# Sending the row of maxima to its place from ScalarE's queue

## The reference

```
h      = group_norm(x)                     # 32 groups of 6 channels, per sample
q,k,v  = h @ qkv_w + qkv_b                 # 12 heads x 16
attn   = (q * 16**-0.5) @ k.T + rel_h + rel_w   # rel_h, rel_w: q times a table, by row and by column
out    = softmax(attn) @ v
x      = x + out @ proj_w + proj_b
```

## Time and profile before

| | |
|---|---|
| median of three runs (lowest to highest) | 3290.96 us (3282.64 to 3295.18) |
| the profiled execution, its time and its span | 3282.28 us, 3280.5 us |
| instructions | 84768 |
| mean granted TensorE clock | 0.743 |
| transfers issued by SP for the row of maxima | 256, of 2.3 KB |

### The profile page before, as it was taken

The page is one execution under the profiler, slowest core; times in us unless marked ns, Lnnn a source line. Parts: engine busy times, 40 slices in busy tenths (PEclk is TensorE's granted clock), DMA queues, the critical chain, the costliest instruction groups (busy, mean ns, idle before and its releaser), DMA issues. The chain is left out here.

```text
span 3280.5 us, 84768 instructions
## 1 busy us (share of the span) xinstructions
PE 2706.0 (82%) x28288; PEld 1964.7 (60%) x28288; DVE 2205.2 (67%) x4041; ACT 2282.8 (70%) x4097; POOL 914.6 (28%) x2052
## 2 busy tenths in 40 slices
PE   2887988888888888878888888788888888888887
PEld 1565655566556656656666566566565655665665
DVE  4666766666666666666776666676667766666775
ACT  2677767767766677667777666777677777667775
POOL 1232222222222232223222222322322222223231
PEclk9877777767766786677677777777777776677787
DMA  2222222222222222222222222222222222222221
GB/s 54 61 76 63 67 70 69 62 65 74 68 62 62 66 76 64 62 66 75 65 75 69 62 67 68 71 61 68 72 65 62 72 71 62 63 67 75 62 76 40
DMA packets 170839, 217.61 MB, mean 66 GB/s; under 512 B 29935, under 2 KB 138220, under 8 KB 170446
## 3 DMA queue, kind: packets, MB, share of 16 engines
q1 hardware_dynamic: 170446, 211.93, 25.5%
HBM read 117.30 MB, written 57.80 MB: 53 GB/s over the span
## 5 line engine op out<-in xcount | busy, mean ns | idle before, releaser
L726 DVE TENSOR_REDUCE mx<-ps_max 98x2 f32<-98x392 f32 x1536 | 827.4, 558 | 515.7 <-PE ps_max L538 503.5
L780 DVE TENSOR_TENSOR rel_hl<-ps_m,rel_hi 64x504 f16<-64x504 f32 (+1 forms) x768 | 938.6, 1222 | 249.1 <-ACT rel_hi L666 232.3
L597 ACT ACTIVATE probs<-ps_sc 98x392 f32<-98x392 f32 x1536 | 739.3, 498 | 245.3 <-PE ps_sc L550 225.0
L569 PE MATMUL ps_o<-probs,v_st 98*32 98x196 f32 x6144 | 540.6, 434 | 268.6 <-ACT o_sb L590 246.2
L666 ACT ACTIVATE rel_hi<-ps_m,is_lo 64x504 f16<-64x504 f32 (+1 forms) x384 | 752.7, 1960 | 4.9
L538 PE MATMUL ps_max<-k_st,q_st 124*98 124x196 f16 x3072 | 660.4, 305 | 101.9 <-issue 91.3
L538 PEld LDWEIGHTS ps_max<-k_st,q_st 124*98 124x98 f16 x3072 | 333.0, 146 | 493.5 <-issue 401.1
L550 PE MATMUL ps_sc<-q_st,k_st 125*98 125x196 f16 x3072 | 626.2, 293 | 1.6 <-DMA q_st<-mrow 1.5
L550 PEld LDWEIGHTS ps_sc<-q_st,k_st 125*98 125x98 f16 x3072 | 411.7, 155 | 5.3 <-DMA q_st<-mrow 2.0
L822 POOL TENSOR_TENSOR xn_lo<-xn,xn_hi 96x392 f16<-96x392 f32 x128 | 118.8, 928 | 1005.3 <-ACT xn_hi L616 1005.3
L569 PEld LDWEIGHTS ps_o<-probs,v_st 98*32 98x32 f32 x6144 | 138.6, 123 | 428.8 <-issue 210.9
(11 more groups left out here) (71 smaller groups left out, 3957.9 us busy)
## 6 DMA issues: line engine op xcount, KB each, us to landing
q_st<-q_dram SPq DMA_DIRECT2D x128, 294.0 KB, 3.9
k_st<-k_dram SPq DMA_DIRECT2D x256, 147.0 KB, 3.0
q_dram<-qk_hl SPq DMA_DIRECT2D x128, 147.0 KB, 2.8
k_dram<-qk_hl SPq DMA_DIRECT2D x128, 147.0 KB, 2.8
q_st<-rel_hl SPq DMA_DIRECT2D x256, 73.5 KB
q_st<-rel_hl SPq DMA_DIRECT2D x256, 64.3 KB
xa<-in_x SPq DMA_DIRECT2D x64, 147.0 KB
xd<-in_x SPq DMA_DIRECT2D x64, 147.0 KB
```

The source lines that it names most:

```text
L569: last = nc.tensor.matmul(ps_o[32 * j:32 * j + 32, 0:TOK], v_st[u.r][:, kt, head_of(head), :], p[:, kt, :], start=kt == 0, stop=kt == 1)
L597: nc.scalar.activation(probs[head][:, :, :], ps_sc[head % 2][0:HT, 0:2 * TOK].rearrange("p (k t) -> p k t", k=2), ACT.Exp, scale=1.0 / (QS ...
L726: nc.vector.reduce_max(mx[u.r % 2][:, s, :], ps_max[s % 2][0:HT, 0:2 * TOK].rearrange("p (q k) -> p q k", q=2), axis=AX.X).then_inc(s_mx, 1)
L780: last = nc.vector.tensor_tensor(l, src, h, ALU.subtract)
```

## The change

The two transfers of `mrow` leave SP's queue. ScalarE issues them itself, right behind the instruction that writes `mrow`, after a wait for that instruction's own semaphore. Source, destination and the semaphores on which the landing is counted are the same. What follows on ScalarE's queue (`rel1` in slot 1, `xT` in slot 6) stands behind the transfer now, and SP no longer waits for `s_mrow`.

```diff
--- before (SP)
+++ after (SP)
-                def maxima(unit_, half):
-                    if active(unit_):
-                        wait(sp, s_mrow, unit_.n * 2 + half + 1)
-                        sp.dma_start(q_st[unit_.r][R_MAX:STACK, half * HH:half * HH + HH, :, :],
-                                     mrow[unit_.r % 2][:, half, :]).then_inc(s_m[half][unit_.r], 16)
...
-                maxima(c, 1)
                 if active(e):
                     wait(sp, s_rlo, e.n * 3 + 3)
...
                 if active(u):
                     wait(sp, s_qklo, u.n * NT + NT)
                     to_dram(u, q_dram, 0, s_qd)
-                maxima(m, 0)
                 if active(u):
                     to_dram(u, k_dram, HQ * HD, s_kd)
--- before (ScalarE)
+++ after (ScalarE)
                             nc.scalar.activation(mrow[u.r % 2][:, half, :], ps_m[BANK[name]][0:HEADS, 0:HT],
                                                  ACT.Copy, scale=-1.0 / KS).then_inc(s_mrow, 1)
+                            act.wait_ge(s_mrow, u.n * 2 + half + 1)
+                            act.dma_start(q_st[u.r][R_MAX:STACK, half * HH:half * HH + HH, :, :],
+                                          mrow[u.r % 2][:, half, :]).then_inc(s_m[half][u.r], 16)
```

## The result

The changed kernel takes 3391.03 us (median of 4 runs, 3381.86 to 3400.09) against 3288.66 us for the kernel before, run beside it: a ratio of 1.0306, 95% interval 1.0269 to 1.0344. The forecast was 3400 us and 1.033. The profiled execution took 3391.8 us with a span of 3390.0 us, 109.5 us over that of before.

The account below looks back on a forecast made before the run. The lead passes between engines within each iteration, with ScalarE leading in slots 0 to 2 almost without cover. 102 us for slot 1 plus 10 for slot 6 makes 112: 3394 us profiled, median 3400, range 3320 to 3480.

Parts of the forecast that it names:

- Where the loss sits: Slots 0 to 2: ScalarE leads, under 0.1 us cover for VectorE, none for TensorE; slot 1 costs 102 us.
- The issue: ScalarE, slot 1: each transfer issue holds its queue 0.80 us, as on SP, delaying everything queued behind it.
- the 102 of the sum: Slot 1 term: 128 units times 0.80 us of issue on ScalarE, 102 us.
- (A): ScalarE's computing isn't held up by the issue; SP's relief is left, median about 3256 us, faster; chance 0.10.
- (B): The issue holds ScalarE only 0.34 us, like `xa`; slot 1 costs 44 us, median about 3322 us; chance 0.12.
- (C): Issue dearer on ScalarE, or waiting for SP's in slot 6: 1.2 us; 3502 us at the end, 3450 middle; chance 0.12.
- The wait: Slot 1, ScalarE's wait for its own `mrow`: costs nothing, since L650 already starts 0.25 us after `mrow`, which takes 0.24.
- Slot 6, ScalarE's side: Slot 6: `xT` starts 0.87 us later, some 0.5 us is left at `vr` and reaches `rel0` of the next iteration.
- Slot 6, SP's side: Slot 6: without the rows SP issues `q_st` 0.57 us earlier; TensorE's wait for it falls from 62.7 to under 30 us.
- the step behind it: End of iteration: an earlier `q_st` saves time in the 86 units that wait, at most 49 us if ScalarE's path stays.
- Rival (D): TensorE's clock returns to the high level 0.8 us later each unit, adding 51 us: 3451 us; chance 0.05.
- +10 us: Slot 6 net: +21 us in 42 units, -20 in 86, put at +10; bounds -49 to +111.

Follow-up runs that it names:

- slot 1 alone: Kernel before with only slot 1's row of maxima (mT1) issued by ScalarE, mT0's row left on SP: 3366.1 against 3267.3 us, ratio 1.0304.
- the changed kernel's second trace: The changed kernel, unaltered, run again on the chip of the experiments against the kernel before: ratio 1.0296.
- slot 6 alone: Kernel before with only slot 6's row of maxima (mT0) issued by ScalarE, mT1's row left on SP: ratio 1.0051, 17 us.
- the doubled issue: The changed kernel plus a second transfer of the same row to a spare tile in slot 1: ratio to before 1.0681, 219 us over.
- Two kernels: Kernel before with k_dram issued behind q_st: ratio 0.9990; the same with both rows of maxima sent from GpSimd's queue: ratio 0.9997.
- The two that shortened it by 56 us: Kernel before, all on SP, with mT0's row issued behind q_st: ratio 1.0021; the same with k_dram behind q_st and the row: 0.9992.
- second comparison: The changed kernel, unaltered, timed once more against the kernel before on the chip of the experiments: ratio 1.0296.

## Why the prediction was right, and where it was not

**Where the loss sits.** Right. ScalarE leads in slots 0 to 2 without cover, slot 1 alone costs 98.9 us, and TensorE's wait for `o_sb` went to 353.9 us where some 340 were forecast.

**The issue.** 0.80 us was taken from SP's rows, 0.73 was measured, and with the wait and what stands around it 0.77 us are lost; 99 us for the 102 of the sum. (A), a ScalarE that is not held up, fell, and so did (B), a cheap issue like `xa`, and (C), a dear one. The Trainium skill's account (Perfetto Trace Analysis, "DMA Instruction — HWDGE (DVE, Sync)") that the sequencer is free only when the descriptors are made fits what the trace shows: L643 starts 0.04 us after the issue of 0.73 us has ended (1635.59 + 0.73, then 1636.36), and a second issue costs as much again. A clash with SP's issues was not seen at the median. The cheapest issue of the trace was not `xa` with 0.33 to 0.34 us but `xd<-in_x` with 0.32; it changes nothing in the sum.

**The wait.** The prediction costed wait and issue separately, the wait at nothing. As a sum that was right, as a mechanism it missed the point. Alone the wait costs nothing (ratio 1.0002), and the issue without a wait for its direct predecessor costs nothing either (0.9990, two instructions further down). Only the pair costs 3%: the wait empties the computing part, and then nothing is there to be worked off while the queue issues. The prediction counted what stands behind the issue and didn't see that what stands ahead of it goes on computing.

**Slot 6, ScalarE's side.** Mis-sized. 0.5 us was forecast at `vr`, 0.16 was measured (0.18 by the medians). `xT` is later as forecast (0.95 us, 1.03 by the medians, forecast 0.87). What was left out is that ScalarE catches up: when its inputs lie ready, one instruction starts before the one before it has ended. After the change `probs`, `o_sb` and the next start 0.38, 0.39 and 0.20 us apart; before, `probs` took its full 0.50 until `o_sb`.

**Slot 6, SP's side.** Wrong. `q_st` was to leave 0.57 us earlier and its wait to fall from 62.7 to under 30 us; it fell to 57.5 (51.0 in the changed kernel's second trace, 38.8 with slot 6 alone). The 0.57 us came from one iteration, 3.37 us from issue to issue, less a median landing. SP's own waits, before and after, say more than that:

```profile
SPq L400 <- DMA q_dram<-qk_hl: 35.7, 55, 1.5
```
```profile
SPq L390 <- DMA q_dram<-qk_hl: 199.9, 128, 3.0
```

Before, SP already stood waiting for `q_dram` to land in 55 of 128 units, and there the rows were not what held `q_st` back; after, it does so in all 128. From the issue of `q_dram` to that of `q_st` the median went from 3.26 to 3.04 us, 0.22 earlier. The page has a landing of 3.0 us for `q_dram` in place of 2.8; that this comes from `k_dram` directly behind it is not shown, since slot 1 alone, with the row still between the two, has 3.0 as well and the doubled issue 2.9.

And the step behind it, that each us of this wait is a us of time, does not hold. Two kernels shortened it by 23 and 26 us without a new wait for the row and measured 0.9990 and 0.9997: TensorE waited for ScalarE instead, and its products in slots 2 to 6 took longer (19.2 and 34.1 us, the first of them near the spread of the traces). (The two that shortened it by 56 us only moved the wait to the row.)

The errors of slot 6 cancel in the sum: +10 us was put down, and 109.5 - 99 = 10.5 us are what the two profiled executions leave. That agreement is luck. Beside 101.2 us in slots 1 to 2 the stretches have 31.6 more in slots 6 to 1 (1551.3 against 1519.7) and 22.7 less in slots 2 to 6 (1185.2 against 1207.9), and the sum has no such terms. The medians of the runs differ by 102.4 us, which leaves 3; the changed kernel in its second comparison costs no more than slot 1 alone; and slot 6 by itself measured 17 us.

**TensorE's clock.** Rival (D) fell, the other way round. The same 28288 products took 2676.6 us in place of 2706.0, at a mean granted clock of 0.757 in place of 0.743. In slots 2 to 6, with idle times of 54.4 and 57.2 us, the products took less time, and that gave a little of the loss back. In a second pair the busy time was 2653.9 us for the changed kernel and 2686.0 for the one with the row behind `rel1`, on one chip. A longer standstill doesn't always bring this: with two issues TensorE stood still longest, and slots 2 to 6 took 1212.8 us. No run here shows what decides it.

No version was found that beats the kernel before. Three that send slot 1's row, or both, from another queue are level with it: in slot 5, behind `rel1`, and from GpSimd.

## What to carry to other kernels

A transfer's issue on a computing engine is not counted as busy, yet it holds all that stands behind it in that queue, here 0.73 us for 2.3 KB; what stands ahead of it computes on. Place it behind an instruction that still has long to run and doesn't feed it, so that the semaphore it waits for comes while there is still work ahead: two instructions further down the same issue was free. A wait of one engine that nearly ties with another path is no reserve: shortening it by 23 and 26 us bought nothing here, and a small transfer moved behind a large one on its queue only gave the wait a new name.

## What was not expected of the hardware

ScalarE's queue runs ahead of its computing part also for transfers. With L649 starting at 1618.90 and still 3.1 us of `rel1` ahead of it in program order, the issue started at 1618.91.

The issue's time doesn't go by the bytes: 0.34 us for 147 KB of `xa`, 0.80 for 2.3 KB that go from 12 partitions to one, 0.73 for the same on ScalarE and 0.546 on GpSimd.
